# Layer 1's experts: results added to the output by scatter on GpSimd, gathers removed, last two attention tiles reordered

## What is computed

```python
x = x + _L1_attn_ref(_layernorm(x), Wq, Wk, Wv, Wo)
def _L1_ffn_ref(x, W_experts, b_experts, W_router, b_router):
    router_weights = softmax(einsum('bsd,ed->bse', x, W_router) + b_router)
    topk_w, topk_idx = top_k(router_weights, 2)        # 2 of 8 experts
    router_weights = zeros.at[b, s, topk_idx].set(topk_w)
    expert_out = einsum('bsd,eod->bseo', x, W_experts) + b_experts
    return einsum('bseo,bse->bso', expert_out, router_weights)
x = x + _L1_ffn_ref(_layernorm(x), ...)
```

## Time and profile before

| | us |
|---|---|
| median of 3 runs (2222.97 to 2227.69) | 2227.19 |
| the profiled execution's own time | 2230.2 |
| its span, first to last instruction | 2228.2 |
| PE busy | 2147.7 (96%) |
| DVE busy | 1078.3 (48%) |
| ACT busy | 329.3 (15%) |
| POOL busy | 274.4 (12%) |
| DMA between HBM and the core, mean | 152 GB/s |

### The profile page before, as it was taken

One profiled execution on the slowest core, in us unless ns is written; L12 is line 12 of the kernel. 1 busy time (PEld: TensorE's weight loads), 2 busy tenths in 40 slices (PEclk: granted clock), 3 DMA queues, 4 the chain that ended last, 5 costly groups with the idle time before them and its releaser, 6 DMA issues.

```text
span 2228.2 us, 47221 instructions
## 1 busy us (share of the span) xinstructions
PE 2147.7 (96%) x18643; PEld 1609.6 (72%) x18643; DVE 1078.3 (48%) x2945; ACT 329.3 (15%) x775; POOL 274.4 (12%) x356
## 2 busy tenths in 40 slices
PE   7999999999889999999998999999999999999798
PEld 7888878888678887888885676676766766556443
DVE  3665434444433333333335565565565565466523
ACT  0000011111111111111111212122111222112110
POOL 0000000211223333333331000000000000001102
PEclk9999999999889999999999999999999999999799
DMA  7334420000289999899994322303213224122234
GB/s 269 93 100 160 121 92 11 19 10 10 103 306 341 330 340 320 305 338 326 341 307 145 123 82 65 118 24 122 104 43 118 71 85 166 52 68 85 74 123 155
DMA packets 95967, 337.87 MB, mean 152 GB/s; under 512 B 17938, under 2 KB 18738, under 8 KB 86528
## 3 DMA queue, kind: packets, MB, share of 16 engines
q1 hardware_dynamic: 66144, 284.16, 35.9%
q0 software_dynamic: 18208, 39.70, 7.2%
q10 hardware_dynamic: 11520, 12.65, 1.7%
HBM read 286.53 MB, written 51.42 MB: 152 GB/s over the span
## 4 chain that ended last, share of the span: by engine, by line
PE 74%; DMA 16%; issue 4%; DVE 2%; POOL 1%; SPq 1%; ACT 1%; DVEq 0%; POOLq 0%; ACTq 0%
DMA x_rows<-work,small 13%; PE psum L403 12%; PE psum L736 10%; PE psum L409 8%; PE psum L758 7%; PE psum L475 7%; PE psum L653 4%; PE psum L882 3%; PE psum L721 3%; PE psum L313 3%; PE psum L798 3%; PE psum L700 3%; PE psum L812 3%; PE psum L770 2%; PE psum L661 2%
## 5 line engine op out<-in xcount | busy, mean ns | idle before, releaser
L653 PEld LDWEIGHTS psum<-work,arena 128*128 128x128 f32 x3072 | 355.2, 193 | 31.7 <-issue 30.8
L653 PE MATMUL psum<-work,arena 128*128 128x128 f32 x3072 | 355.7, 276 | 1.4 <-ACT work L1839 1.4
L403 PE MATMUL psum<-work,arena 128*128 128x128 f32 x2560 | 296.6, 279 | 5.0 <-DVE work L1108 2.1
L403 PEld LDWEIGHTS psum<-work,arena 128*128 128x128 f32 x2560 | 294.2, 195 | 7.2 <-issue 3.7
L1972 POOL TENSOR_TENSOR small<-small 128x1 f32<-128x1 f32 x143 | 62.2, 435 | 1807.4 <-issue 826.2
L736 PE MATMUL psum<-work,arena 128*128 128x257 f32 x1024 | 234.1, 381 | 2.3 <-ACT work L1878 1.6
L736 PEld LDWEIGHTS psum<-work,arena 128*128 128x128 f32 x1024 | 189.7, 190 | 32.5 <-issue 4.5
L1714 ACT COPY work<-psum 128x512 f32<-128x512 f32 (+1 forms) x182 | 95.6, 547 | 772.2 <-PE psum L313 693.0
L409 PE MATMUL psum<-arena,work 128*128 128x512 f32 x448 | 201.3, 602 | 0.7 <-ACT work L1714 0.7
L661 PE MATMUL psum<-arena,work 128*128 128x512 f32 x384 | 181.9, 611 | 0.0
L758 PE MATMUL psum<-work 128*128 128x512 f32 x384 | 169.2, 593 | 0.0
(11 more groups left out here) (235 smaller groups left out, 2333.7 us busy)
## 6 DMA issues: line engine op xcount, KB each, us to landing
arena<-in_experts SPq DMA_DIRECT2D x64, 2304.0 KB, 9.7
expert_rows<-work SPq DMA_DIRECT2D x8, 2304.0 KB, 10.5
work<-in_ctxT SPq DMA_DIRECT2D x32, 514.0 KB, 4.7
work<-in_ctx SPq DMA_DIRECT2D x32, 512.0 KB, 4.1
work<-in_ctx_tail SPq DMA_DIRECT2D x32, 450.0 KB, 3.2
work<-last_key_probs ACTq DMA_DIRECT2D x32, 256.0 KB, 3.7
arena<-in_experts SPq DMA_DIRECT2D x8, 1024.0 KB, 5.4
arena<-in_qkv SPq DMA_DIRECT2D x1, 6144.0 KB, 19.1
```

The source lines that it names most:

```text
L403: done = nc.tensor.matmul(to[:, n * P:(n + 1) * P], w[:, j, at:at + P], src[:, j * P:(j + 1) * P], start=(j == 0), stop=(j == KD - 1))
L653: done = nc.tensor.matmul(to[:, n * P:(n + 1) * P], w[:, at:at + P], xgT[e % 2][:, j * P:(j + 1) * P], start=(j == 0), stop=(j == KD - 1))
```

## The change

- A row in `expert_rows` gets two more values: its token's number and the weight of this choice (`RW` = 514 words, 2056 B). The two scatters of a tile need different weights, so the second reads from `xw`, a copy of the rows that ACT makes (`copy_rows`). Rows that no token fills hold the number 4096 (`NOWHERE`), out of range.
- Biases are added to `x` of tiles 0 to 6 before the blocks, and SP stores these tiles in the output then.
- DVE takes a block's result times the weight in the row. POOL adds it to the output by a scatter with addition, with the row numbers from the row itself. Each scatter waits until the one before has landed.
- The store of block results, the result places, the 14 gathers and `combine` are gone.
- A block's rows are loaded when the block four before has been added, a result is taken when the block three before has been.
- The end of the attention is written in another order: tile 6 is projected out and chosen ahead of tile 7's scores, and the table of blocks is made before tile 7 is added to `x`. Tile 7's own choice moves behind block 0. The eight whole products stand one behind each of the blocks 6, 8, ... 20.

```diff
+WHOLE_ROWS, SHARES_AT, BIAS_AT = 0, 4, 5
+WHOLE_AFTER = (6, 8, 10, 12, 14, 16, 18, 20)
+RW = D + 2
...
             def take_block(k):
                 if k >= len(yk):
-                    dve.wait_ge(s_y1[k % len(yk)], 16 * (k // len(yk)))
-                dve_take(dve, c, lambda src: nc.vector.tensor_copy(yk[k % len(yk)], src))
+                    dve.wait_ge(s_added, 16 * (k - len(yk) + 1))
+                dve_take(dve, c, lambda src: nc.vector.tensor_scalar(yk[k % len(yk)], src, xgk[k % AHEAD][:, D + 1:D + 2], None,
+                                                                     ALU.mult))
...
+            pool.wait_ge(s_rows_out, 16 * SPARSE)
+            for k in range(BLOCKS1):
+                pool.wait_ge(s_proj_free, taken0 + evicted(k))
+                hold()
+                pool.wait_ge(s_added, 16 * k)
+                pool.indirect_dma_start(t["out"], bass.IndirectOffsetOnAxis(ap=xgk[k % AHEAD].bitcast(U32)[:, D:D + 1], axis=0),
+                                        yk[k % len(yk)], None, bounds_check=B * S - 1, oob_is_err=False,
+                                        compute_op=ALU.add).then_inc(s_added, 16)
+            pool.wait_ge(s_added, 16 * BLOCKS1)
...
             def load_block(k):
                 if k >= AHEAD:
-                    sp.wait_ge(s_tp, turned0 + k - AHEAD + 1 + (k >= AHEAD + 2))
+                    sp.wait_ge(s_added, 16 * (k - AHEAD + 1))
                 sp.dma_start(xgk[k % AHEAD], xs_d[bass.ds(rows[k], P), :]).then_inc(s_xg1[k % AHEAD], 16)
             for k in range(AHEAD):
                 load_block(k)
-            for k in range(BLOCKS1):
-                if k + AHEAD < BLOCKS1:
-                    load_block(k + AHEAD)
-                sp.wait_ge(s_proj_free, taken0 + k + 1)
-                sp.dma_start(y_d[k * P:(k + 1) * P, :], yk[k % len(yk)]).then_inc(s_y1[k % len(yk)], 16)
             for i in range(SPARSE):
-                sp.wait_ge(s_final, i + 1)
-                sp.dma_start(t["out"][i * P:(i + 1) * P, :], x[:, i * D:(i + 1) * D]).then_inc(s_out, 16)
+                sp.wait_ge(s_bias_taken, i + 1)
+                sp.dma_start(t["out"][i * P:(i + 1) * P, :], x[:, i * D:(i + 1) * D]).then_inc(s_rows_out, 16)
+            for k in range(AHEAD, BLOCKS1):
+                load_block(k)
```

More of the change, by code:

```diff
@@ L379, in positions_in_experts, with count_chosen @@
             pe_project(pe, c, emit)
+        def count_chosen(pe, c):
+            c.sel1.add()
+            wait(pe, s_sel1, c.sel1.value())
+            pe_project(pe, c, lambda to: nc.tensor.matmul(to[:, 0:EXPERTS1], ones1, cumb1, start=True, stop=True))
         def attention_pe(pe, st, c, following=None, entered=False):
@@ L904, in moe1_pe @@
             where = [pe.snap(r, min_val=0, max_val=(EXPERTS1 - 1) * W1) for r in registers]
+            pe.wait_ge(s_wmat, 1)
+            pe_transpose(pe, c, [wmat[:, j * P:(j + 1) * P] for j in range(2)])
+            wait(pe, s_tp_free, c.tp.value())
+            for i in range(SPARSE):
+                bias(i)
             turned = turn_block(0)
@@ L1911, in take_block @@
                 act_take(act, c, xgkT[k % 2])
-            for part in range(2):
-                act_take(act, c, xn2T[:, part * 2 * P:(part + 1) * 2 * P])
-            c.route.add()
-            wait(act, s_logit, c.route.value())
-            nc.scalar.activation(prob1, logit1, ACT.Exp, bias=top, accum_out=rsum).then_inc(s_exp, 1)
+            act_take(act, c, wT)
             take_block(0)
```

337 lines of the change are left out of this document (162 added, 175 removed).

## The result

| | before | after |
|---|---|---|
| median | 2227.44 us (4 runs, 2222.97 to 2232.44) | 2252.11 us (4 runs, 2244.95 to 2260.05) |
| the profiled execution's own time | 2230.2 us | 2249.65 us |
| its span | 2228.2 us | 2247.6 us |
| mean granted clock of TensorE | 0.982 | 0.983 |

The ratio is 1.0089, with a 95% interval of 1.0060 to 1.0118: the changed kernel is slower by 0.9%, some 20 us (the medians of these four runs each lie 24.7 apart), and outside the range of the prediction (2221 to 2242).

The account below looks back on a forecast made before the run. TensorE bounds the blocks, with some 6 us of gathers and additions behind. TensorE's end 2222.0 plus 4.1 tail and 3.2 scatters gave span 2229.3; by the median 2228.3, plus 0.2 contention, 2228.5; range 2221 to 2242.

Parts of the forecast that it names:

- at nothing: Changes costed at zero: ScalarE's second row copy, 2056 B rows (0.4% more load bytes, under 3.8 us matmul), weight in the take.
- Tail removed: Behind TensorE's last product: store, 14 gathers and 14 additions go; 4.1 us in place of 9.4, worth 5.3 us.
- The reorder: End of attention, before the blocks: finishing tile 6 first brings the block table at 2096.6 against 2106.8, 10 us gained.
- The low clock: TensorE before block 0, after gaps: 3.4 us once; the last output projection also slowed, to 6.71 us.
- The register load: Before block 0: the 21-register load lies hidden under TensorE's wait for VectorE's four bias additions; no time of its own.
- The work behind block 0: TensorE after block 0: 20 blocks, eight whole products, tile 7's rows; 106.9 us, ending at 2222.0 against 2218.8.
- The scatters with addition: In the blocks: a full block lands in 4.8 us, 5.5 in the chain; TensorE loses 3.2 us in all.
- The rivals: Three alternatives in the last 170 us: scatter chain slower, 0.27; TensorE earlier, 0.22; clock falling among the blocks, 0.08.
- The chain sets the end: In the blocks: full scatter landings from about 5.5 us outpace TensorE; 5.8 taken, time 2238; chance 0.27.
- TensorE bounds and starts earlier: Before and in the blocks: no small-matmul gaps, half the clock cost, cheap scatters; time 2219 to 2223; chance 0.22.

## Why the prediction was wrong

The forecast was 2228.5 and the measurement 2252.1. What failed is one sentence of the part "at nothing": "the rows of 2056 B in place of 2048 add 0.4% to loads that land under 3.8 us of matmul". It counted bytes, and it looked at the loads of the blocks alone. The same `RW` sets the width of the eight clears, eight times 2313 KB, and the sentence does not have them. What the runs showed in its place: the clears land in 13.7 us in place of 10.5, A to B takes 20.9 us more, and the clears alone, put into the kernel before, bring the whole loss (ratio 1.0107). Both the part and the list of rivals stayed inside the last 170 us, "the only part in which the change moves the end". That choice of stage was the real error: it named the stage by where the change is spoken of, not by what its sizes touch.

Step by step, from TensorE's last projection of queries and keys, which started at 2056.62 before and at 2074.47 after:

```profile
2056.62 6.98 PE psum L409 x16
```

```profile
2074.47 6.98 PE psum L414 x16
...
2150.26 4.92 DMA out<-work
```

| us behind that point | predicted | after |
|---|---|---|
| block table there | 40.0 | 38.8 |
| last output projection ends | 41.8 | 40.1 |
| block 0 ends | 58.5 | 58.9 |
| TensorE ends | 168.6 | 168.8 |
| span ends | 172.7 | 173.1 |

- **Tail removed**: right. 4.3 us behind TensorE's last product, 4.1 predicted, 9.4 before. The end is set by the last tile's store, as forecast.
- **The reorder**: right in its sum. The table is 11.0 us earlier seen from C (10.2 predicted). The low clock came where it was expected: the last output projection took 6.12 us, and the granted clock is 0.50 (1.2 GHz) in 2100 to 2110 and in 2120 to 2130, 0.67 between, where TensorE was busy 37, 70 and 52%.
- **The register load**: wrong, and hidden by other errors. I had laid it under the wait for VectorE's additions. Its price, 5.17 us, stood in the trace of before and was not read. After, it left TensorE idle for 4.76 us, and the additions behind it for another 2.55. Biases 4 to 6 began 50.6 us behind the last projection, 49.5 predicted, though the table was 1.2 us and the projection 1.7 us earlier than forecast. From there to block 0's end it took 8.3 us where 9.0 had been allowed, so block 0's end came out within 0.4 us all the same. That is luck.
- **The work behind block 0**: right in its sum; TensorE needs 110.0 us, 110.1 predicted. The parts differ: 1.8 us of it are waits for rows, 3.2 predicted, and the rest is 1.3 us longer than the 106.9 of the forecast.
- **The scatters with addition**: right in the landing, too high in the stall. Full blocks land in 4.7 to 4.9 (4.8 predicted), starts are 5.7 us apart in a row (5.5), the stall falls on the rows of blocks 6 and 7, 1.31 and 0.51 us, where one of 3 us was forecast. With plain scatters the stretch from E on was 2.8 us shorter. So the landings of layer 0 were the right row, and the rule of the Trainium skill, DMA: Bandwidth & Descriptors, section Anatomy of one DMA, which names no extra for addition, was not: 4.7 against 2.7 us in the same place of the program.
- **The rivals**: none of the three was what happened. "The chain sets the end" was the slower one and would have been 2238 with landings of 5.8 us; landings stayed under 5.0. "TensorE bounds and starts earlier" did not occur either: block 0 ended 58.9 us behind the point, not earlier than forecast. The blocks ran at a granted clock of 0.99 to 1.00.

So from the last projection on the change costs 1.5 us by the traces, with 1.1 forecast. The match is in part luck: measured from the last eight of these products, the stretch takes 162.4 to 164.2 us in the six traces of the old order. The 21 us came from a place to which no step was given.

## What to carry to other kernels

When a change widens a row by a few bytes, list every DMA that uses that width, all through the program, and ask of each where its rows start: a pitch of 2056 B made writes to DRAM 30 to 46% slower here, pitches of 2080 and 2112 B did not, and 14 words of padding undid the loss from A to B. Ask next whose small, awaited DMA is issued while the large one runs, since that wait, not the bytes, is what TensorE paid here, and moving the large one by one step was worth as much as making it fast. And look up the rows of register loads: one of 21 registers took 5.2 us on TensorE's queue, unseen as long as products were queued ahead of it. Put it under a long run of products, or load only what the next block needs.

## What the runs showed of the hardware

- Writes of 1152 rows to DRAM: 10.5 us with rows of 2048 B at multiples of 2 KB, 10.9 with a pitch of 2080 B, 11.2 with 2112, 13.7 to 15.3 with 2056 (12.4 to 12.7 where the clears were moved). With the start of every row off by 8 B the kernel lost 1.7 times as much in the stage as with 2056 B (39.3 against 23.7 us).
- A scatter with addition of 128 rows of 2 KB lands in 4.7 us where the plain one takes 2.7, and is issued in 1.55 us in place of 0.99. A block with one filled row landed in 2.8.
- A load of 21 registers takes TensorE 5.2 us in the ten kernels that have it ahead of the bias products or under whole products (5.4 and 7.85 us in the two that have it among the bias products) and SyncE 1.65 us in before. One register took TensorE 0.48 us, five 0.92, fifteen 3.81.
- What stays open: whether the slow rows are read, changed and written again in DRAM or lose their time elsewhere. No run here looked at that, nor at starts off by 16 B. Why one load of 21 registers took 7.85 us is open too. Nor is it settled how much of the medians' 5 us between like kernels comes from the stages ahead of A, whose length varied by 22 us between the traces.
